# A two-layer decoder: the five engines' meeting after the expert layer replaced by waits, and eight bias products moved to the other bank

## What is computed

```python
x = _layernorm(x + _L0_attn_ref(x, ...))          # gated state-space mixer
x = _layernorm(x + _L0_xattn_ref(x, ctx_1024, ...))  # cross attention
x = _layernorm(x + _L0_ffn_ref(x, ...))           # experts, 2 of 16
x = _layernorm(x + _L1_attn_ref(x, ...))          # time mixing, channel mixing
x = _layernorm(x + _L1_xattn_ref(ctx_1024, x, ...))
x = _layernorm(x + _L1_ffn_ref(x, ...))           # experts, 6 of 32, anchors
```

```python
logits = jnp.einsum('bsd,de->bse', tensor, Wr) + br
probs = jax.nn.softmax(logits, axis=-1)
topv, topi = jax.lax.top_k(probs, NUM_SELECTED)
gate = jnp.sum(jax.nn.one_hot(topi, NUM_BANKS, dtype=tensor.dtype) * topv[..., None], axis=-2)
h = jax.nn.relu(jnp.einsum('bsd,edh->bseh', tensor, W1) + b1)
y = jnp.einsum('bseh,ehm->bsem', h, W2) + b2
out = jnp.einsum('bse,bsem->bsm', gate, y)
```

## Time and profile before

| | |
|---|---|
| median of 3 executions | 1708.89 us |
| lowest and highest | 1707.06 and 1710.91 us |
| time of the profiled execution | 1705.89 us |
| its span in the trace | 1704.1 us |
| TensorE busy | 1435.7 us, 84% |
| VectorE / ScalarE / GpSimd busy | 889.7 / 583.8 / 531.4 us |
| bank stage, about | 370 to 735 us |
| mix stage, about | 745 to 980 us |

### The profile page before, as it was taken

The page is one execution under the profiler, slowest core; times in us unless marked ns, Lnnn a source line. Parts: engine busy times, 40 slices in busy tenths (PEclk is TensorE's granted clock), DMA queues, the critical chain, the costliest instruction groups (busy, mean ns, idle before and its releaser), DMA issues.

```text
span 1704.1 us, 29292 instructions
## 1 busy us (share of the span) xinstructions
PE 1435.7 (84%) x10056; PEld 1108.3 (65%) x10056; DVE 889.7 (52%) x2529; ACT 583.8 (34%) x1449; POOL 531.4 (31%) x515
## 2 busy tenths in 40 slices
PE   7768997559999999946999879988888666999987
PEld 3455676448888889933666535665555444899975
DVE  7353556522121212239876236667768742666656
ACT  4204443201112112213333225443434312666652
POOL 2011000012222222111333211133435474666775
PEclk9898999679999999967999979999999887999999
DMA  7771000078777879511000071112222699655528
GB/s 222 191 247 51 2 15 14 25 282 315 288 275 278 313 288 325 207 50 34 16 0 1 0 177 35 50 61 81 91 81 103 206 323 335 181 174 169 165 64 344
DMA packets 133602, 258.94 MB, mean 152 GB/s; under 512 B 13898, under 2 KB 106216, under 8 KB 127184
## 3 DMA queue, kind: packets, MB, share of 16 engines
q1 hardware_dynamic: 111328, 210.89, 37.4%
q0 software_dynamic: 17520, 39.88, 6.6%
q10 hardware_dynamic: 4608, 6.29, 1.2%
HBM read 197.71 MB, written 52.72 MB: 147 GB/s over the span
## 4 chain that ended last, share of the span: by engine, by line
PE 49%; DVE 9%; issue 8%; POOL 6%; DMA 4%; SPq 2%; ACT 1%; POOLq 1%; ACTq 0%; DVEq 0%
PE bank L152 45%; POOL xe L1655 4%; PE bank L2199 2%; DMA arena<-in_banka 1%; DMA arena<-yr 1%; SPq L2377 1%; DVE arena L1953 1%; DVE arena L197 1%; SPq L2406 1%; DVE arena L1943 1%; POOLq L165 1%; DVE arena L1124 1%; DMA arena<-xd,arena 1%; SPq L2378 1%; PE bank L1233 1%
## 5 line engine op out<-in xcount | busy, mean ns | idle before, releaser
L152 PE MATMUL bank<-arena 128*128 128x128 f32 (+8 forms) x8728 | 1290.0, 337 | 154.4 <-DMA arena<-in_banka 22.9
L152 PEld LDWEIGHTS bank<-arena 128*128 128x128 f32 (+5 forms) x8728 | 965.7, 181 | 433.0 <-issue 274.6
L1124 DVE TENSOR_SCALAR arena<-bank,arena 128x128 f32<-128x128 f32 x188 | 52.9, 344 | 285.8 <-PE bank L152 285.8
L2340 POOL DMA_INDIRECT yr<-arena x159 | 169.6, 1066 | 94.8 <-ACT arena L2270 51.2
L190 POOL TENSOR_TENSOR arena<-arena 128x1 f32<-128x1 f32 (+1 forms) x48 | 37.4, 780 | 331.9 <-DVE arena L182 331.9
L1151 POOL DMA_INDIRECT arena<-xd,arena x47 | 45.7, 972 | 275.4 <-PE bank L1079 240.2
L1655 POOL DMA_INDIRECT xe<-arena x112 | 113.0, 1009 | 31.6 <-issue 31.6
L2305 DVE COPY arena<-arena 128x768 f32 x127 | 76.1, 599 | 58.3 <-issue 58.2
L1102 ACT ACTIVATE arena<-bank 128x256 f32<-128x256 f32 x47 | 18.0, 383 | 230.5 <-PE bank L152 230.5
L1855 ACT ACTIVATE arena<-bank,arena 128x256 f32<-128x256 f32 x128 | 58.9, 472 | 97.9 <-DVE arena L1943 97.9
L1111 ACT ACTIVATE arena<-bank,arena 128x128 f32<-128x128 f32 x188 | 53.6, 368 | 92.7 <-PE bank L152 92.7
(11 more groups left out here) (259 smaller groups left out, 1444.8 us busy)
## 6 DMA issues: line engine op xcount, KB each, us to landing
arena<-in_bank SPq DMA_DIRECT2D x47, 2052.0 KB
arena<-xe SPq DMA_DIRECT2D x159, 129.0 KB, 2.3
arena<-kd SPq DMA_DIRECT2D x16, 1024.0 KB, 10.9
arena<-arena SPq DMA_DIRECT2D x16, 896.0 KB, 5.3
arena<-in_bank SPq DMA_DIRECT2D x8, 1536.0 KB, 12.7
arena<-yr SPq DMA_DIRECT2D x16, 768.0 KB, 15.5
xe<-arena SPq DMA_DIRECT2D x1, 6321.0 KB, 29.7
arena<-in_ctx SPq DMA_DIRECT2D x8, 512.0 KB, 4.2
```

Of the source, the lines that this page charges most:

```text
L152: return t.matmul(o, l, r, start=start, stop=stop, skip_group_check=True)
L1124: h = v.tensor_scalar(h_ring[i % 3][:, (4 + m) * 128:(5 + m) * 128], banks[b][:, m * 128:(m + 1) * 128], sbc(w_ring[i % 5], 4100 + m), 0.0 ...
L2340: p.indirect_dma_start(yr, bass.IndirectOffsetOnAxis(ap=sidx.bitcast(I32)[:, n:n + 1], axis=0), y2_ring[n % NY], None, bounds_check=14335, ...
```

## The change

It has two parts. First, the meeting of all engines between the bank and the mix stage is gone (the one after the mix takes its number). In its place ScalarE and VectorE call the new `experts_over` ahead of their first instruction of the mix: they wait for the last `l2` product and for all scatters. TensorE, GpSimd and SyncE get no wait there. Second, a bias product goes to bank (k + 1) % 2 instead of k % 2. All eight are in even steps, so from bank 0 to bank 1.

```diff
                 for p2 in biases_at(k):
                     t.wait_ge(late_in, 64)
-                    b, n = use(("b2", p2), k % 2)
+                    b, n = use(("b2", p2), (k + 1) % 2)
                     t.wait_ge(bank_free[b], n)
...
+        def experts_over(e):
+
+            b, n = U["l2", NT0 - 1]
+            e.wait_ge(bank_full[b], n + 1)
+            for j in range(3):
+                e.wait_ge(y_out[j], 16 * len(range(j, NT0, 3)))
+
         def scalar_mix(a):
+            experts_over(a)
...
         def vector_mix(v):
+            experts_over(v)
...
             tensor_bank(t)
+            tensor_mix(t)
             barrier(t, 4)
-            tensor_mix(t)
-            barrier(t, 5)
             tensor_second(t)
```

More of the change, by code:

```diff
@@ L2439, in _ @@
             scalar_bank(a)
+            scalar_mix(a)
             barrier(a, 4)
-            scalar_mix(a)
-            barrier(a, 5)
             scalar_second(a)
@@ L2457, in _ @@
             vector_bank(v)
+            vector_mix(v)
             barrier(v, 4)
-            vector_mix(v)
-            barrier(v, 5)
             vector_second(v)
@@ L2472, in _ @@
             gpsimd_bank(p)
+            gpsimd_mix(p)
             barrier(p, 4)
-            gpsimd_mix(p)
-            barrier(p, 5)
             gpsimd_second(p)
@@ L2486, in _ @@
             sync_bank(s)
+            sync_mix(s)
             barrier(s, 4)
-            sync_mix(s)
-            barrier(s, 5)
             sync_second(s)
```

## The result

| | before | changed |
|---|---|---|
| median | 1709.39 us (4 executions) | 1686.61 us (4 executions) |
| lowest and highest | 1707.06, 1710.91 | 1685.28, 1690.37 |
| profiled execution: time, span | 1705.89, 1704.1 | 1690.37, 1688.5 |
| changed / before | | 0.9871, 95% interval 0.9852 to 0.9891 |

The kernel became 22.8 us faster. The forecast was 1685 us, with 1678 to 1693 as its range. The time lies inside, but one of the two parts gave nothing, which the profile of the changed kernel already shows.

The account below looks back on a forecast made before the run. TensorE was taken as the bound, busy 84% of the span, with stalls in the bank stage and a hole at the seam. 11.9 + 6.8 + 5.0 = 23.7 us off the median 1708.9 gave 1685 us, range 1678 to 1693.

Parts of the forecast that it names:

- Eight stalls, 11.9 us: Bank stage: TensorE's eight waits for VectorE's copy of bank 0 ahead of the bias products go, 11.9 us on the path.
- The wait doesn't come back, and the weights suffice: Bank stage: over 4 us of cover keeps bank 1 free for the next transposes; weight loads keep pace, costed at nothing.
- Four falls, 6.8 us: Bank stage: four of eight steps behind a stall run at clock 0.83, 1.69 us longer each; all four falls go.
- no step without a stall shows one: Bank stage, 375 to 735 us: the ground for taking the clock's falls to go with the stalls.
- The restart, 0 to 3.3 us: Bias steps: TensorE's restart after standing still might cost up to 8 x 0.41 = 3.3 us; taken as 0.
- the 0.41 us that I set apart: Bias step: of its 1.29 us over a step without bias, up to 0.41 us might be the engine's restart.
- The seam, 5.0 us: Between bank and mix stage: without GpSimd's drain the sum starts at 742.6 instead of 747.6 us, bound by its load.
- the meeting behind the mix stays, so later stages only start earlier: After the mix: the kept meeting was assumed to add no cost, so the seam's 5.0 us carry through.
- the seam gives nothing: Rival: GpSimd or the load holds VectorE until 747.6 us; gain 18.7, time 1690 us; chance 0.07.

Follow-up runs that it names:

- e_changed_again: The changed kernel run once more, unaltered, beside the version with an extra GpSimd drain at the mix's start: 0.9907 of before, 1691.1 us.
- e_nodrain: The changed kernel, but GpSimd reaches the meeting behind the mix by an empty instruction with the signal, without a drain: 0.9852 of before, 1685.7 us.
- e_stall8: The changed kernel with eight stalls put back, two steps away from the bias products: 0.9959 of before, on a slower chip.
- e_bias: The kernel before with only the bias products moved to the other bank, the meeting left in: 0.9863 of before, 1688.3 us.
- e_seam: The changed kernel with the bias products back in bank 0, so only the meeting is replaced by waits: 0.9988 of before, 1708.4 us.
- e_early: The changed kernel with one more GpSimd drain, without signal, at the start of its part of the mix: 0.9837 of before, 1683.8 us.
- e_rows128: The kernel before, stalls kept, each bias product replaced by a stand-in with 128 rows of weights (identity times wfv): 1701.8 us in one execution.
- e_stall_all: The changed kernel with a stall in every step from 4 on, 45 in all: 1836.4 us in one execution, on a chip that ran before at 1772.2.

## Why the prediction was right, and where it wasn't

- **Eight stalls, 11.9 us: right.** From the first bias product to ScalarE's last copy the stage took 360.4 us before and 342.8 after, 17.5 less. Seven stalls (10.5), four falls (6.8) and 0.04 us per step (0.3) make 17.6. The eighth stall, 1.4 us, lies before the first product. It is gone too, but in the trace of the changed kernel the 1.6 us of low clock shown above took its place; without them the bank stage is 357.9 us in `e_changed_again` and 357.2 in `e_nodrain`. One reading of mine was loose: the earlier trace rows are only the longest pieces of the chain. Between them, ahead of each bias product, VectorE's relu and copy stand in it, which is the stall itself.
- **The wait doesn't come back, and the weights suffice: right.** TensorE's one gap is at the start, and loads at 299 GB/s for the whole stage (from 282) kept up.
- **Four falls, 6.8 us: the size is right, the reason only half.** The step "no step without a stall shows one" took the stall as the cause. It was the stall together with the bias products behind it: stalls alone had none of 8, the stand-in of 128 rows behind a stall none of 8, products of 16 rows without a stall none of 8. Either part's removal gives the 6.8 us back. The number isn't fixed: 4, 5 and 4 of 8 in three traces. The passage from the Trainium skill ("TensorE: Matmul & The Clock Gate", "A second HAM failure mode: psum-queue depth-cycling") gave the right sign, but `e_stall8` has small gaps too, 8 of 1.4 us, and its clock stayed up.
- **The restart, 0 to 3.3 us: 0 was right.** A bias step is 8.50 us without a stall and 8.54 with one. Of the 0.41 us that I set apart, 0.04 went with the stall and 0.19 with the 16 rows (or with the operands): behind a stall, the stand-in of 128 rows takes 8.35 us. The rest is what my estimate of a record was short by.
- **The seam, 5.0 us: right at its place, wrong in the sum.** The sum started 4.03 us behind its load, 5.01 us earlier than before relative to the last copy, to 0.1 us what was worked out. The step that failed is "the meeting behind the mix stays, so later stages only start earlier". I had read 8.97 us for the drain and said that no row tells on what. I asked whether it would hold GpSimd's next instruction, and not who would drain GpSimd next. What it measured is 5.4 us lost there, against the 5.0 won. The trace of before had the hint, in the view of line 165 shown above: of its five drains of GpSimd, the one at the seam took 8959 ns and the last, behind the mix, 1 us, having nothing to pay. The rival "the seam gives nothing" named the right size, 1690, with another mechanism.
- **The median.** By the rows alone the gain is 17.6 + 5.1 - 5.7 (mix and next seam) = 17.0 us (the spans differ by 15.6, since the changed kernel's bank stage happened to start 1.6 us later), and by the medians 22.8, 22.1 in `e_bias` and 18.0 in `e_changed_again`. The rows set the kernel before at its fastest, 1705.9 us, against the changed one at its slowest, 1690.4. The others of before may have had more than four falls, at 1.7 us each, as the trace of `e_seam` with five and 1711.6 us has it, but no second trace of before shows that; the rest of the difference is open. So it was partly luck that the forecast came as close as it did: the 5.4 us that went missing were made up by the spread between executions.

## What to carry to other kernels

A drain can be a debt: taking a meeting away removes its drain, but what that drain waited for may fall due at the next one, on the path again. Look for the next drain of the same engine and put an extra one where the engine idles; here, by the rows, it cost nothing and was worth 5.4 us. When a wait for a PSUM bank is found, look at what takes the bank before it in the same step: choosing the other one gave all of this change.

## What the runs showed of the hardware that wasn't expected

- GpSimd's drain behind 94 indirect DMAs took 8.97 us, although all of them had landed 6.6 us before its end, and 8.82 us when it came 240 us later. Further ones took 2.6 to 11.5 us, of which 0.5 to 4.2 behind the last packet of GpSimd's DMA queue, more with more DMAs since the last drain; one right behind another took 53 ns. An instruction on data, or a signal without a drain, didn't wait for it (`e_early`, `e_nodrain`).
- Products of the same columns took longer with 16 rows of weights than with the stand-in's 128: a step behind a stall, at full clock, 8.54 against 8.35 us. The operands differed too.
- A stall of 1.5 us lowered TensorE's clock in 4 to 5 of 8 cases with 16-row products behind it, and in none of 8, 8 and 37 with full ones (`e_stall8`, `e_rows128`, `e_stall_all`): from 2.4 to 1.2 GHz for part of the step, 1.7 us each.
